# A decoder layer on one core: fillers ahead of the first transposes, another order of the first panels' reads, one narrow job moved, and another order at the start of the experts

## What is computed

```python
x = x + attn(layernorm(x), Wq, Wk, Wv, Wo)
#   q = rope(h @ Wq)  k = rope(h @ Wk)  v = h @ Wv      32, 8 and 8 heads of 128
#   softmax(causal(q k^T / sqrt(128))) v @ Wo
x = x + fake_quant(layernorm(x)) @ fake_quant(ctx)      # clip(round(x / s + z), 0, 255)
#   the same for ctx, 1024 x 1024 for each of the two batches
x = x + experts(layernorm(x))
#   gate = softmax(top 16 of 64 (h @ Wr.T @ keys.T));  z = (h @ A.T) * gate;  out = z @ B.T * 2
```

## Time and profile before

| | us |
|---|---|
| three runs | 1324.74, 1323.55, 1320.39 |
| median | 1323.55 |
| the profiled execution, its own time | 1322.61 |
| its span, first to last instruction | 1320.8 |
| TensorE busy | 1269.2 (96%) |
| VectorE, ScalarE, GpSimd busy | 818.0, 770.2, 602.1 |
| mean granted TensorE clock | 0.992 |

### The profile page before, as it was taken

How to read it: one execution, slowest core, us unless ns; L and a number is a source line. 1 busy time by engine, 2 the same in 40 slices (tenths; PEclk the granted TensorE clock), 3 DMA queues, 4 the chain that set the end, 5 groups by cost and what they waited for, 6 DMA issues and landing times. The chain is left out here.

```text
span 1320.8 us, 19919 instructions
## 1 busy us (share of the span) xinstructions
PE 1269.2 (96%) x7025; PEld 1091.4 (83%) x7025; DVE 818.0 (62%) x1798; ACT 770.2 (58%) x1582; POOL 602.1 (46%) x446
## 2 busy tenths in 40 slices
PE   5879999999999999999999999999999999988998
PEld 5758998888888888888888888888888887766887
DVE  7788224555555555555555655655787788777663
ACT  4411137777767767777777867863333355555540
POOL 4665666777767777687667745420000000020100
PEclk9999999999999999999999998999999999999999
DMA  7033134646849659477386578758964486100001
GB/s 270 17 120 120 65 123 149 184 128 191 232 127 237 195 142 275 134 172 207 93 232 168 133 214 262 210 187 256 283 197 132 151 287 200 58 1 17 33 33 48
DMA packets 117122, 207.42 MB, mean 157 GB/s; under 512 B 10128, under 2 KB 51088, under 8 KB 113440
## 3 DMA queue, kind: packets, MB, share of 16 engines
q1 hardware_dynamic: 112992, 176.79, 40.7%
q0 software_dynamic: 4032, 29.36, 12.0%
HBM read 147.40 MB, written 88.08 MB: 178 GB/s over the span
## 5 line engine op out<-in xcount | busy, mean ns | idle before, releaser
L1235 DVE TENSOR_TENSOR pT_lo<-banks,pT_hi 128x512 fp32r<-128x512 f32 (+1 forms) x192 | 103.7, 595 | 179.2 <-ACT pT_hi L970 179.1
L1634 PE MATMUL banks<-ob_hi,oa_hi 128*128 128x512 f32 x384 | 149.7, 390 | 0.9 <-DVE ob_lo L1272 0.9
L1634 PE MATMUL banks<-ob_hi,oa_lo 128*128 128x512 f32 x384 | 149.6, 390 | 0.0
L1634 PE MATMUL banks<-ob_lo,oa_hi 128*128 128x512 f32 x384 | 149.6, 389 | 0.0
L1592 PE MATMUL banks<-xc,nring_hi_a 128*128 128x512 f32 x448 | 140.2, 394 | 1.2 <-DVE q_made L1185 1.2
L1592 PE MATMUL banks<-xc,nring_hi_b 128*128 128x512 f32 x448 | 139.9, 394 | 0.0
L954 ACT CAST oa_hi<-oraw 128x1024 fp32r<-128x1024 f32 x48 | 50.5, 1052 | 142.7 <-PE banks L1634 133.1
L970 ACT CAST pT_hi<-banks 128x512 fp32r<-128x512 f32 (+1 forms) x192 | 86.5, 526 | 75.9 <-PE banks L1562 75.8
L1833 POOL TENSOR_TENSOR resid<-resid,colterm 128x1024 f32<-128x1024 f32 x8 | 19.1, 2382 | 223.7 <-ACT colterm L1891 137.6
L1244 DVE CUSTOM_DVE_ANT_0 prob<-banks,mask 128x512 f32<-128x512 f32 (+3 forms) x256 | 109.8, 485 | 0.3 <-DVE resid L1163 0.3
L728 POOL TENSOR_TENSOR q_lo<-q_raw,q_hi 128x512 fp32r<-128x512 f32 x64 | 86.7, 1356 | 40.7 <-ACT q_hi L907 40.6
(11 more groups left out here) (245 smaller groups left out, 3450.4 us busy)
## 6 DMA issues: line engine op xcount, KB each, us to landing
q_raw<-qk_dram SPq DMA_DIRECT2D x64, 256.0 KB, 4.1
o_S<-o_st SPq DMA_DIRECT2D x64, 256.0 KB, 3.9
w<-in_L_attn_Wo SPq DMA_DIRECT2D x32, 512.0 KB, 5.4
oraw<-o_S SPq DMA_DIRECT2D x32, 512.0 KB, 3.8
nraw<-in_L_attn_Wq SPq DMA_DIRECT2D x28, 512.0 KB, 5.5
o_S<-o_S POOLq DMA_DIRECT2D x12, 1024.0 KB, 10.0
o_S<-o_N POOLq DMA_DIRECT2D x12, 1024.0 KB, 10.2
resid<-in_x SPq DMA_DIRECT2D x16, 512.0 KB, 7.7
```

The costliest lines, as they stand in the source:

```text
L1235: nc.vector.tensor_tensor(pT[1][:, sl], turned_chunk(turned, mixed, c), as32(pT[0][:, sl]), ALU.subtract).then_inc(pT_lo, 1)
L1634: ins = nc.tensor.matmul(step_bank(m, t), oa[a][:, s % 2, k, t * P:(t + 1) * P], ob[c][:, s % 2, k, :], start=(q == 0 and k == 0 and i == ...
```

## The change

1. **Fillers.** 72 transposes of the unit matrix into bank 7 stand ahead of the first fills on TensorE; nothing reads them.
2. **t1 on GpSimd.** The four differences `t1` move from VectorE to GpSimd, behind the weight sum S3 and ahead of `w_low(4)`; each now waits for all of `t3`. S3 waits for a normalised tile in place of `t1`, `w_low(4)` for all of `t2`, and `t2` waits no more for `w_low(4)`.
3. **Order of VectorE's reads** in panels 0 and 1: `c00(1, fb)` goes between panel 0's sums, and the sums and `keep_u` of panel 1 go between the turns of panel 0.
4. **PLACES.** Unit 55 has one job, so the last job, 111, is at (56, 0). `load_first(0)` and `load_first(1)` stay in unit 56 (their condition is rewritten), and `turn_added` of the last job stands behind the other work of its place on GpSimd.
5. **Experts' start.** `turn_quantised(2)` and `(3)` go earlier on TensorE, `late_stats` and `late_scale` earlier on VectorE, `gate(0)` ahead of `scale_of(2)`, in tile 1 `exponentials` and the casts ahead of `copy_turned(4)` on ScalarE, and `add_out` in two halves with the casts' differences between them.
6. `TURNED` becomes a tuple of the panels (0, 1) that are rotated; the panels themselves stay as they were.

```diff
+WARM = 72
+
-                     for p in ((0, 1, 2) if u in (3, 5, 8, 12, 16) else (0,) if u in (50, 52) else (0, 1))]
+                     for p in ((0, 1, 2) if u in (3, 5, 8, 12, 16) else (0,) if u in (50, 52, 55) else (0, 1))]
...
-            if u == LAST_JOB_UNIT + 1:
+            if u == LAST_JOB_UNIT:
                 load_first(0)
...
+        def t1(t):
+            pool.wait_ge(t3_sum, TPB)
+            nc.gpsimd.tensor_tensor(right(t, 0), right(t, 0), left(t, 0), ALU.subtract).then_inc(t_sum, 1)
+
...
         w_low(3)
-        pool.wait_ge(t_sum, TPB)
+        pool.wait_ge(ln_out_v, 5)
         weight_sum(0, "S3")
+        for t in range(TPB):
+            t1(t)
+        pool.wait_ge(t_sum, 2 * TPB)
         w_low(4)
         for t in range(TPB):
             t4(t)
...
-            if (u - 1, 0) in JOB_AT:
+            if (u - 1, 0) in JOB_AT and u - 1 < LAST_JOB_UNIT:
                 turn_added(JOB_AT[u - 1, 0])
...
+            if u == LAST_JOB_UNIT:
+                turn_added(JOBS - 1)
             for f in steps_of(u + 1):
                 first_low(f)
...
-            if s >= 1:
+            if s >= 2 or s == 1 and which == 3:
                 dve.wait_ge(made, tile_no(s - 1, {2: "C01", 3: "C11"}[which], fb) + 1)
...
         keep_u(0, 2, 0)
+        c00(1, 0)
         keep_u(0, 2, 1)
+        c00(1, 1)
         keep_u(0, 3, 0)
         keep_u(0, 3, 1)
         c11(0, 0)
         c11(0, 1)
-        c00(1, 0)
-        c00(1, 1)
         c10(0, 0)
         c10(0, 1)
-        c11_turns(0)
-        c01(0, 0)
+        c01_sum(0, 0)
+        c11_turn(0, 0)
+        c01_sum(0, 1)
         keep_u(1, 2, 0)
-        c01(0, 1)
+        c11_turn(0, 1)
         keep_u(1, 2, 1)
+        c01_turn(0, 0)
+        keep_u(1, 3, 0)
+        c01_turn(0, 1)
+        keep_u(1, 3, 1)
...
+        for n in range(WARM):
+            nc.tensor.transpose(banks[:, 7, 0:P], ident[:], ident[:])
         fills(range(8))
...
+        late_root(0)
         root(1)
         highs("b", range(2, 4))
         read_product(2)
         normalise(1)
         highs("b", range(4, 6))
+        copy_turned(3)
         root(2)
-        copy_turned(3)
-        late_root(0)
         exponentials(0)
...
-            if i == 1:
-                copy_turned(i + 3)
             exponentials(i)
             if i + 1 < TT:
                 highs("x", (2 * i + 2, 2 * i + 3))
+            if i == 1:
+                copy_turned(i + 3)
...
             gate(i)
+            add_out(i - 1, 0)
             if i + 1 < TT:
                 lows("x", (2 * i + 2, 2 * i + 3))
-            add_out(i - 1)
+            add_out(i - 1, 1)
...
-        turn_fills("a", range(5, 8))
+        turn_fills("a", range(5, 7))
         turn_quantised(2)
+        turn_fill("a", 7)
         turn_fills("x", range(2))
...
             if i == 0:
                 turn_fills("b", range(4, 6))
+                turn_quantised(3)
```

More of the change, by code:

```diff
@@ L1358, in _ @@
             t3(t)
-        for t in range(TPB):
-            t1(t)
         for f in range(8, 16):
@@ L2058, in _ @@
         row_term(0)
+        late_stats(TPB)
         add_product(0)
```

89 lines of the change are left out of this document (45 added, 44 removed).

## The result

The changed kernel takes 1303.64 us (median of 4 runs, 1302.38 to 1304.59), the one before 1322.62 us beside it (4 runs, 1320.39 to 1324.74). The ratio is 0.9856, 95% interval 0.9837 to 0.9876: 1.4% faster. The profiled execution spans 1302.8 us, 18.0 less than the 1320.8 of before, and the forecast was 1306.

What follows compares the result with a forecast made beforehand. TensorE was taken as the bound, busy 1269.2 of 1320.8 us, leaving about 50 us idle plus slow pace behind pauses. Terms 2.8 + 8.7 + 1.0 + 4.1 = 16.6 us off 1322.6 gave 1306.0 us, range 1299 to 1312.

Steps and rivals of the forecast that it cites:

- fillers: Kernel start: 72 fillers bring TensorE to full pace, ending near 12.8 us; first product at 18.2 us, 1.1 us won.
- t1 on GpSimd, contention off: Ahead of the projections: low parts come 2.5 us earlier without t1 on VectorE, less 0.8 us for S3 beside t3.
- panels 0 and 1: Projections: VectorE's new order removes 10.0 us lost, adds 1.3 us of new waits; 8.7 us won, ends 4 and 10.
- last narrow job: Units 55 and 56: job 111 at (56, 0) fills one wait, unit 55 gains one; 1.0 us won, ends -2 and 4.
- experts: Experts' start: 1.0 us at tile 2, 3.1 us at tile 4's multiply; sum 4.1 us, ends 1 and 7.
- Rival (b): Kernel start: fillers don't raise the pace or run slowly to the end; fills 4.7 us late, 1312 us; chance 0.07.
- the charge for S3 beside t3: Before the projections: GpSimd's S3 (2.37 us), starting near 31 us, reaches into VectorE's t3 and costs 0.8 us.
- The rule cited in the prediction: VectorE with two SBUF inputs contends with GpSimd reading SBUF; the second to issue waits for the whole of the first.
- two late `keep_u(1, 3, ·)`: Panel 1: these stand behind a turn each and come 0.4 and 0.9 us late for P4, 1.3 us of waits.
- Rival (a): The second panel's stall only shrinks; panel gain 4 us instead of 8.7, 1311 us; chance 0.12.
- rival (c): No low clock around units 56 to 58 and in the experts: 4 and 7 us won, 1300 us; chance 0.11.
- rival (d): Panel 1: w_low(9) from GpSimd comes late and VectorE stands with all turns; 1327 us at 20 us late; chance 0.02.

Runs made afterwards that it cites:

- fill_0: The changed kernel without the 72 filler transposes ahead of the first real one; 1306.38 us, 0.9881 of before.
- t1_dve: The changed kernel with the t1 differences back on VectorE and GpSimd's S3 behind the first of them, as before; 1305.26 us, 0.9874 of before.
- panel_old: The changed kernel with VectorE's old order in panels 0 and 1; 1311.55 us, 0.9927 of before.
- units_old: The changed kernel with the last narrow jobs, load_first and turn_added placed as before; 1303.05 us, 0.9853 of before.
- experts_old: The changed kernel with the experts' old start on ScalarE, VectorE and TensorE; 1308.39 us, 0.9897 of before.
- low_first: The changed kernel with the first step's low half (L801) ahead of the last narrow job's turn on GpSimd; 1304.77 us, 0.9859 of before.
- fill_36: The changed kernel with 36 filler transposes instead of 72; 1306.58 us, 0.9888 of before.
- scale_late: The changed kernel with the low halves of tile 1 ahead of scale_of(2) on VectorE; 1301.83 us, 0.9841 of before.

## Why the prediction held, step by step

Forecast 1306.0, range 1299 to 1312, measured 1303.64.

| term | forecast | between the traces | by taking it out |
|---|---|---|---|
| fillers | 1.1 | 1.33 | 1.6 (fill_0, at the long run) |
| input earlier | 0 | 0.36 | 0 |
| t1 on GpSimd, contention off | 1.7 | 1.3 | 1.3 (t1_dve) |
| panels 0 and 1 | 8.7 | 9.4 | 10.7 (panel_old) |
| last narrow job | 1.0 | 2.1 | 1.0 (units_old) |
| experts | 4.1 | 3.8 | 4.6 (experts_old) |
| sum | 16.6 | 18.3 | |

The sum of the third column is 0.3 us more than the 18.0 of the spans; that much is lost in drifts between the places. Taken out one by one the parts come to 19.2 us; 1.2 of that is panel_old's longer stretch at half clock.

**Fillers.** They were to end near 12.8 us and ended at 13.14; the first product was to come at 18.2 and came at 17.60, with 0.36 us from the input. The mechanism was right. That the end came out near the forecast is partly luck: it took 17 fillers at half pace, the changed kernel had 23, and the others with 72 had 15 to 28. At 28 the fillers ended at 13.56 and 13.64 us and just touched the work, so 72 is about as many as fit. Rival (b) did not occur.

**t1.** Forecast 2.8 us for start and move together, measured 2.98. Inside it the charge for S3 beside t3 was too small, 0.8 against 1.11 us: t3 could start at 31.97 us, where the forecast's own times (33.67 less 1.1) give 32.6, and more of S3 was left. The rule cited in the prediction has the right form: t3 stood until S3 was over. The fillers' surplus of 0.2 us and the earlier input cover it. The prediction found that the two rows agree with the rule in their sum more than in their length. With the GpSimd row ahead of them they agree in length as well:

```profile
807.53 1.27 POOL L794 TENSOR_TENSOR oa_lo<-oraw,oa_hi 128x512 fp32r<-128x512 f32 x1 [7.53 <-ACT oa_hi L938]
```

VectorE's L1258 started at 808.43 us, and this instruction ended at 808.80: L1258 ended at 809.89, the 1.22 us that it takes alone less 0.13 behind that. GpSimd's next, started at 808.99, ended at 811.02, its own 1.27 us less 0.14 behind 809.89. Each stood until the other was over.

**Panels.** `keep_u(1, 2, 0)` was to come near 83 us and came at 82.90; the panel's end was to be near 109 and was 107.80. Of the two late `keep_u(1, 3, ·)`, 1.3 us together, 0.42 was left, all of it at one place. Rival (a), a stall that only shrinks, did not occur; panel_old shows that nothing else in the change removes it.

**Last narrow job.** The forecast of 1.0 us net agrees with units_old, but its parts don't. `turn_probs(55)` waits 1.32 us instead of 1.6. `turn_probs(56)` waits not at all, where 1.5 to 3 us were to be left. In exchange the first step waits 2.06 us for L801, which the forecast didn't see (low_first, where L801 stands ahead of the turn, has no such wait): it named what is queued on SyncE behind `load_first(1)`, not that on GpSimd the last turn now stands ahead of `first_low(0)`. The two misses cancel, so that the size of this term came out right by luck. What was won is the half clock and not the wait (units_old), and the clock there is chance in part: it read 1.00 throughout this place in the changed kernel, as rival (c) had it, but fell in four of the ten kernels with the same code at this place, at a cost of 1.5 us in fill_36 and about 0.1 us in the other three.

**Experts.** 3.27 us of the 3.8 are tile 4's multiply, whose wait of 3.12 us is gone as forecast. At `hidden(1)` the forecast had `scale_of(2)` eat the gain of tile 3. It does more than that: the gain up to there is 16.84 - 14.17 = 2.67 us, of which 1.03 us goes in the longer wait and 1.07 in the longer stretch at half clock behind it. The step priced the wait and not the clock. But the 1.07 us of clock may be chance, since three of the ten traces with the changed kernel's pauses lost no more than the kernel before. By scale_late both together cost 1.0 to 2.9 us.

The remaining 1 us between forecast and median is the base: the 18.0 us off the profiled 1322.6 would give 1304.6.

One sum of the prediction mixes its bases: rival (d) at 20 us late is 1326 us by the profiled 1322.6 us, and 1327 only by the median. Nothing rests on it.

## What to carry over

A stall behind one engine's queue is removed by an order in which each result stands just ahead of its reader, and it is found by laying the queue against the reader's times: that was worth 9 of 18 us and was forecast within 0.7. After an edit ask of every queue, GpSimd's and ScalarE's too, what now stands ahead of the next urgent instruction; the wait for L801 and the one ahead of `hidden(1)` were such places. Behind a long pause of TensorE the half clock cost 1.4 to 2.7 us more in most of these runs and nothing in one, so a pause is to be priced with it, as a range, and a few small instructions in front of the awaited one are worth moving. One trace of each kernel can't tell such a gain from a lucky clock; the same place in all the other traces can.
